# First attention stage: 16 heads in pairs on different row and column groups of TensorE

## The chip, the cores and the metric

One Trainium2 chip, one of its cores. The metric is the device time of one execution in microseconds, the median of several runs.

## What is computed

All tensors are fp32. The reference has two layers, cut here to what matters:

```python
# layer 0: x, ctx are (32, 256, 256); 16 heads of 16 features
q, k, v = x @ Wq.T, ctx @ Wk.T, ctx @ Wv.T      # split in 16 heads
att = softmax(q @ k.T * 16 ** -0.5) @ v          # per head, heads put side by side
x = x + att[0]                                   # of batch 0 alone, added to all 32
# layer 1, for each of the 32 batches
nX, nF = layernorm(ctx) * w1 + b1, layernorm(x) * w2 + b2
A = softmax(nF @ nX.T / 16) @ nX
c = gelu(A @ fc1.T + b) @ fc2.T + b
n = layernorm(c) * w3 + b3
out = nF + gamma2 * (c + gamma1 * softmax(n @ n.T / 16) @ n)
```

Of layer 0 only batch 0's attention is needed. It has 16 heads, 256 queries and 256 keys.

## The kernel before

Each engine runs a program written out by hand, and semaphores tie them together. No scheduler moves anything. There are five stages, one after the other:

- projections q, k, v of batch 0 (L700, L706);
- the first stage proper, the 16 heads of batch 0 (L719 to L755 on PE, L370 to L392 on DVE, L571 to L586 on ACT). It ends in tgt2, the attention's result;
- the second stage over 32 batches: POOL adds tgt2 to each x tile (L310) and normalizes (L317), PE transposes (L768) and multiplies (L778, L785, L794, L806);
- a short stretch on DVE (L486 to L501), then the second attention over 16 pairs of batches (L839 to L895);
- the output (L914, L554) and its stores.

In the first stage proper one head goes through five steps. **Scores**, L725: two fp32 matmuls, one for each half of the queries. The head's 16 features lie in a group of 32 partitions: heads h and h + 1 (h even) share a group, and kTm holds k twice, once with the even heads' features zeroed and once with the odd ones'. So a score matmul uses 32 rows of the array and all 128 columns. The result, 128 x 512, fills bank 3 or bank 4 of PSUM. **Maximum**, L375 on DVE, into hmax. **Exponential**, L580 on ACT, two instructions into E. **Transposes**, L735: four on PE, over the whole array, into bank 5 or 6, which then are copied to PT by ACT (L586, even heads) or DVE (L381, odd heads). **Output product**, L745: two fp32 matmuls over 128 rows and 32 columns, v1 against PT. Head h writes 32 partitions of bank 0 or 1: partition group h % 4, so the heads of a group of four lie in different column groups of the array.

PE's order sets the pace: in turn h it computes the scores of head h, the transposes of head h - 1 and the output product of head h - 2. The semaphores are s0_mm (scores ready), max0_ok, exp0_ok (two for each head), p0_mm (transposes ready), pt0_ok (two: ACT's and DVE's copy to PT done) and o0_mm (output product done). E, hmax and PT have two buffers each, one for a head.

The second attention (L881) has output products of the same form as L745: fp32, 128 rows, 32 columns, 256 columns moved. Batch 0 of a pair uses column group 0, batch 1 group 1, with a transpose (L851) between them except in the last two pairs. Its scores (L842) are bf16, and the two batches of a pair lie on rows 0 to 35 and 64 to 99 of the array.

Of the kernel before, what the change touches and what calls it, by code (L numbers as in the profile page):

```python
# [24 lines left out]
ALU = mybir.AluOpType  # L25
ACT = mybir.ActivationFunctionType
AX = mybir.AxisListType

P = 128
B = 32  # L30
N = 256
D = 256
NT = N // P
DC = D // P
TILES = B * NT
NH = 16
# [4 lines left out]
VW = 32  # L41
# [7 lines left out]
SU = 6 * U  # L49
CO = 2 * H + 2  # L50
SC = 6 * CO


COLS = {}
# [8 lines left out]
def build(nc, x, ctx, x0t, c0t, wqt, wkt, wvt, params, out):  # L63
    stack = ExitStack()

    def sb(name, shape, dt=F32):
        return stack.enter_context(nc.sbuf_tensor(name, shape, dt))
# [5 lines left out]
    bank = [stack.enter_context(nc.psum_tensor(f"bank{i}", [P, 512], F32)) for i in range(8)]  # L73

    def tiles(ap, w=256):
        return ap[:, 0:2 * w].rearrange("p (a b) -> p a b", a=2)
# [3 lines left out]
    ident = sb("ident", [P, P])  # L80
# [7 lines left out]
    qT = sb("qT", [P, 2, N])  # L88
    kTm = sb("kTm", [P, 2, 2, N])
    v1 = sb("v1", [P, NT, NH, VW])  # L90
    hmax = sb("hmax", [P, 2, NT])
    hsum = sb("hsum", [P, NT, NH])
    tgt2 = sb("tgt2", [P, NT, D])

# [11 lines left out]
    E = sb("E", [P, 2, NT * N])  # L106
    PT = sb("PT", [P, 2, NT * N])
# [37 lines left out]
    PT2 = sb("PT2", [P, 2, 2, NT * N])  # L145
# [17 lines left out]
    consts = sem("consts")  # L163
    q_mm, k_mm, v_mm = sem("q_mm"), sem("k_mm"), sem("v_mm")
    qT_ok, kT_ok, v1_ok = sem("qT_ok"), sem("kT_ok"), sem("v1_ok")
    s0_mm, max0_ok, exp0_ok = sem("s0_mm"), sem("max0_ok"), sem("exp0_ok")
    p0_mm, o0_mm = sem("p0_mm"), sem("o0_mm")
    oT_ok = [sem("oT_first"), sem("oT_second")]
    ot_mm = sem("ot_mm")
    pt0_ok = [sem("pt0_even"), sem("pt0_odd")]  # L170
# [9 lines left out]
    alg = sem("alg")  # L180
# [29 lines left out]
    def phase2(eng, step, last):  # L210
        for p in range(4):
            step(p, p % 2)
        with eng.Fori(2, PAIRS // 2 - 2) as g:
            step(g * 2, 0)
            step(g * 2 + 1, 1)
        for p in range(PAIRS - 4, last):
            step(p, p % 2)

    def paired(p, k):

# [11 lines left out]
    ALG = {}  # L232
# [90 lines left out]
    def _(dve):  # L323
# [43 lines left out]
        dve.wait_ge(qk_mm, 1)  # L367
        link(dve.tensor_copy(Q[:, :], bank[7][:, 0:(H + 1) ** 2]))
        link(dve.tensor_copy(K[:, :], bank[7][:, 64:64 + U * U]), "QK")
        for h in range(NH + 1):  # L370
            if h < NH:
                dve.wait_ge(s0_mm, h + 1)
                if h >= 2:
                    dve.wait_ge(exp0_ok, 2 * (h - 1))
                dve.tensor_reduce(hmax[:, h % 2, :], tiles(bank[3 + h % 2]), AX.X, ALU.max, negate=True)\  # L375
                    .then_inc(max0_ok, 1)
            if h >= 1 and (h - 1) % 2 == 1:
                dve.wait_ge(p0_mm, h)
                if h >= 3:
                    dve.wait_ge(o0_mm, h - 2)  # L380
                dve.tensor_copy(PT[:, (h - 1) % 2, :], bank[5 + (h - 1) % 2][:, :]).then_inc(pt0_ok[1], 1)  # L381
        dve.wait_ge(o0_mm, NH)
        dve.tensor_copy(oT[:, 1, :], bank[1][:, :]).then_inc(oT_ok[1], 1)
        dve.wait_ge(ot_mm, 1)
        for t in range(NT):
            o = bank[5 + t][:, :].rearrange("p (h k) -> p h k", h=NH)
            dve.reciprocal(hsum[:, t, :].unsqueeze(2), o[:, :, DK:DK + 1]).then_inc(hsum_ok, 1)
        for t in range(NT):
            o = bank[5 + t][:, :].rearrange("p (h k) -> p h k", h=NH)
# [172 lines left out]
    def _(act):  # L562
# [5 lines left out]
        for t in range(NT):  # L568
            act.activation(v1[:, t, :, 0:DK], bank[2][:, t * D:(t + 1) * D].rearrange("p (h k) -> p h k", h=NH),
                           ACT.Copy).then_inc(v1_ok, 1)  # L570
        for h in range(NH + 1):  # L571
            if h == 12:
                act.wait_ge(o0_mm, NH // 2)
                act.activation(oT[:, 0, :], bank[0][:, :], ACT.Copy).then_inc(oT_ok[0], 1)
            if h < NH:
                act.wait_ge(max0_ok, h + 1)
                if h >= 2:
                    act.wait_ge(p0_mm, h - 1)
                for t in range(NT):
                    act.activation(E[:, h % 2, t * N:(t + 1) * N], bank[3 + h % 2][:, t * N:(t + 1) * N], ACT.Exp,  # L580
                                   bias=hmax[:, h % 2, t:t + 1]).then_inc(exp0_ok, 1)
            if h >= 1 and (h - 1) % 2 == 0:
                act.wait_ge(p0_mm, h)
                if h >= 3:
                    act.wait_ge(o0_mm, h - 2)
                act.activation(PT[:, (h - 1) % 2, :], bank[5 + (h - 1) % 2][:, :], ACT.Copy).then_inc(pt0_ok[0], 1)  # L586

        def step(i, j, g):
            n = (j + 1) % 2
# [98 lines left out]
    def _(pe):  # L688
# [3 lines left out]
        for c in range(DC):  # L692
            last = pe.matmul(bank[6][:, 0:H + 1], meanw[:, :], a5[:, c, :], start=c == 0, stop=c == DC - 1)
        last.then_inc(mean_mm, 1)

        for arrived, n, w, src, b, done in ((q_in, 32, wqT, x0T, 0, q_mm), (k_in, 32, wkT, c0T, 1, k_mm)):
            pe.wait_ge(arrived, n)
            for o in range(2):
                for c in range(DC):
                    last = pe.matmul(bank[b][:, o * N:(o + 1) * N], w[:, c, o * P:(o + 1) * P], src[:, c, :],  # L700
                                     start=c == 0, stop=c == DC - 1)
            last.then_inc(done, 1)
        pe.wait_ge(v_in, 16)
        for t in range(NT):
            for c in range(DC):
                last = pe.matmul(bank[2][:, t * D:(t + 1) * D], c0T[:, c, t * P:(t + 1) * P], wvT[:, c, :],  # L706
                                 start=c == 0, stop=c == DC - 1)
# [3 lines left out]
        for dst, w, src, n in ((0, meanw, prodQ, (H + 1) ** 2), (64, scalew, prodK, U * U)):  # L711
            for c in range(DC):
                last = pe.matmul(bank[7][:, dst:dst + n], w[:, :], src[:, c, :], start=c == 0, stop=c == DC - 1)
# [2 lines left out]

        pe.wait_ge(qT_ok, 1)
        pe.wait_ge(kT_ok, 2)
        for h in range(NH + 2):  # L719
            if h < NH:  # L720
                o, q, e = h // 8, 32 * ((h % 8) // 2), h % 2
                if h >= 2:
                    pe.wait_ge(exp0_ok, 2 * (h - 1))
                for t in range(NT):
                    last = pe.matmul(bank[3 + h % 2][:, t * N:(t + 1) * N], qT[q:q + 32, o, t * P:(t + 1) * P],  # L725
                                     kTm[q:q + 32, e, o, :], start=True, stop=True)
                last.then_inc(s0_mm, 1)
            if 1 <= h <= NH:
                pe.wait_ge(exp0_ok, 2 * h)
                if h >= 3:  # L730
                    pe.wait_ge(pt0_ok[(h - 1) % 2], (h - 1) // 2)
                n = (h - 1) % 2
                for k in range(NT):
                    for t in range(NT):
                        last = pe.transpose(bank[5 + n][:, k * N + t * P:k * N + (t + 1) * P],  # L735
                                            E[:, n, t * N + k * P:t * N + (k + 1) * P], ident[:, :])
                last.then_inc(p0_mm, 1)
            if h >= 2:
                if h == 2:
                    pe.wait_ge(v1_ok, 2)  # L740
                    pe.wait_ge(consts, 11)
                pe.wait_ge(pt0_ok[h % 2], h // 2)
                group, row = (h - 2) // 4, VW * ((h - 2) % 4)
                for k in range(NT):
                    last = pe.matmul(bank[group // 2][row:row + VW, (group % 2) * N:(group % 2 + 1) * N],  # L745
                                     v1[:, k, h - 2, :], PT[:, h % 2, k * N:(k + 1) * N],
                                     start=k == 0, stop=k == NT - 1, skip_group_check=True)
                last.then_inc(o0_mm, 1)

        for group in range(NH // 4):  # L750
# [65 lines left out]
        for c in range(DC):  # L816
            last = pe.transpose(bank[5][:, c * P // 2:(c + 1) * P // 2].bitcast(BF16),
                                stR[:, c, :, :].rearrange("p m r -> p (m r)"), identb[:, :])
# [156 lines left out]
```

## Time and profile before

| | us |
|---|---|
| median of 3 runs | 375.85 |
| the 3 runs | 373.79, 375.85, 382.89 |
| span of the profiled execution | 371.2 |
| of it: load and projections, to 12.9 | 12.9 |
| the 16 heads, and tgt2 | 48.2 |
| second stage, to about 247 | 185.9 |
| the rest | 124.2 |

The span runs from the first instruction to the last. Of the profiled execution the profile gives the span alone, no other time, so what lies around it is the distance from the span to the three runs. A granted clock of 1.00 is 2.4 GHz on TensorE, 0.50 is 1.2 GHz.

### The profile page before, as it was taken

Reading aid. Unit: us, or ns where it says so; the run is one execution under the profiler, and the core shown is the slowest. Engines: PE = TensorE matmul, PEld = TensorE weight load, DVE = VectorE, ACT = ScalarE, POOL = GpSimd, SP = SyncE. Lnnn points to the kernel's source line nnn. Section 1 sums busy time; section 2 is a strip of 40 time slices with the busy share of each in tenths; the row PEclk is TensorE's granted clock in tenths of the full one; section 3 lists DMA queues with packets and bytes.
Section 4 is the critical chain, followed back from the end, with each engine's and each line's share of the span. In section 5 each row is a group of like instructions: output and inputs, shape, how many; then the busy total and the mean of one; then the engine's idle time right before and its main releaser. Section 6 shows DMA issues by size and latency. Waiting matters only on the chain.

```text
span 371.2 us, 6844 instructions
## 1 busy us (share of the span) xinstructions
PE 297.3 (80%) x1854; PEld 218.2 (59%) x1854; DVE 242.0 (65%) x756; ACT 166.5 (45%) x401; POOL 117.1 (32%) x183
## 2 busy tenths in 40 slices
PE   6899994277989999999999999950049999963683
PEld 5655552166879999998999899950014444421120
DVE  7534345578977778777777773239954666647685
ACT  2334430053566566666566666540054565423340
POOL 9000002664476666666667774000000000000000
PEclk9889998569699999998999899965556999995555
DMA  7300000134414445544444421100000000000798
GB/s 243 127 2 0 0 4 0 42 112 158 172 68 147 145 152 170 170 170 170 170 154 141 150 93 57 58 1 0 0 2 0 1 0 0 2 0 2 266 336 303
DMA packets 19313, 35.10 MB, mean 95 GB/s; under 512 B 2272, under 2 KB 2272, under 8 KB 19296
## 3 DMA queue, kind: packets, MB, share of 16 engines
q1 hardware_dynamic: 19296, 34.89, 26.7%
q8 instruction: 8, 0.13, 0.2%
q14 instruction: 9, 0.07, 0.1%
HBM read 18.11 MB, written 8.39 MB: 71 GB/s over the span
## 4 chain that ended last, share of the span: by engine, by line
PE 25%; issue 24%; POOL 18%; DVE 18%; DMA 10%; SPq 2%; ACT 2%; POOLq 1%; DVEq 0%; ACTq 0%
PE bank L881 7%; POOL zc L317 6%; POOL xN L310 6%; POOL zy L317 6%; DMA xN<-x 5%; DMA out<-fin 4%; PE bank L778 4%; PE bank L858 3%; PE bank L806 2%; DVE bn L427 2%; PE bank L842 2%; PE bank L768 2%; DVE fin L554 2%; PE bank L785 1%; PE bank L830 1%
## 5 line engine op out<-in xcount | busy, mean ns | idle before, releaser
L310 POOL TENSOR_TENSOR xN<-xN,tgt 128x512 f32<-128x512 f32 x32 | 40.5, 1266 | 107.8 <-DVE rstd L401 52.7
L778 PE MATMUL bank<-XT,FT 128*128 128x256 f32 x256 | 66.1, 405 | 0.0
L608 ACT ACTIVATE E<-bank,nmax 128x256 f32<-128x256 f32 x64 | 27.2, 485 | 60.9 <-DVE nmax L458 60.9
L778 PEld LDWEIGHTS bank<-XT,FT 128*128 128x128 f32 x256 | 49.9, 206 | 6.3
L596 ACT ACTIVATE FT<-bank,par 128x256 f32<-128x256 f32 x64 | 32.8, 569 | 24.6 <-PE bank L768 24.2
L427 DVE BATCH_NORM_STATS2 bn<-cN 128x6 f32<-128x256 f32 x64 | 24.1, 418 | 21.2 <-POOL xN L310 21.0
L785 PEld LDWEIGHTS bank<-fc1s,XT 128*128 128x128 f32 x256 | 34.1, 194 | 6.0 <-DVE V L463 4.2
L768 PE MATMUL bank<-ident,zc 128*128 128x128 f32 x128 | 22.2, 299 | 18.5 <-POOL zy L317 12.4
L317 POOL TENSOR_SCALAR zc<-cN,nmean,rstd 128x256 f32<-128x256 f32 x64 | 34.8, 553 | 3.6 <-DVE rstd L401 3.6
L317 POOL TENSOR_SCALAR zy<-xN,nmean,rstd 128x256 f32<-128x256 f32 x64 | 35.0, 557 | 0.0
L785 PE MATMUL bank<-fc1s,XT 128*128 128x4 f32 x256 | 31.0, 244 | 3.4 <-DVE V L463 3.4
L601 ACT ACTIVATE XT<-bank,b1s,w1s 128x256 f32<-128x256 f32 x64 | 32.9, 578 | 0.0
L806 PEld LDWEIGHTS bank<-V,PT 128*128 128x128 f32 x256 | 32.3, 198 | 0.5 <-issue 0.4
L806 PE MATMUL bank<-V,PT 128*128 128x5 f32 x256 | 31.8, 248 | 0.4 <-DVE OA L467 0.4
L881 PE MATMUL bank<-PT,uS 128*32 128x256 f32 x128 | 30.7, 401 | 0.0
L458 DVE TENSOR_REDUCE nmax<-bank 128x2 f32<-128x512 f32 x32 | 21.9, 684 | 10.9 <-PE bank L778 9.3
L375 DVE TENSOR_REDUCE hmax<-bank 128x2 f32<-128x512 f32 x16 | 11.1, 691 | 26.2 <-PE bank L725 26.1
L515 DVE TENSOR_REDUCE nm<-bank 128x2 bf16<-128x512 f32 x32 | 20.6, 685 | 11.2 <-PE bank L842 11.2
L768 PEld LDWEIGHTS bank<-ident,zc 128*128 128x128 f32 x128 | 16.0, 161 | 20.0 <-POOL zy L317 16.0
L830 PE MATMUL bank<-identb,sU 128*128 128x128 bf16 x64 | 7.2, 243 | 24.8 <-ACT sU L630 24.8
L554 DVE TENSOR_TENSOR fin<-bank,Fall 128x512 f32<-128x512 f32 x32 | 21.4, 690 | 7.6 <-DMA out<-fin 4.6
L580 ACT ACTIVATE E<-bank,hmax 128x256 f32<-128x256 f32 x32 | 13.4, 470 | 25.7 <-DVE hmax L375 25.7
(150 smaller groups left out, 494.2 us busy)
## 6 DMA issues: line engine op xcount, KB each, us to landing
cN<-ctx SPq DMA_DIRECT2D x32, 256.0 KB, 2.6
xN<-x SPq DMA_DIRECT2D x32, 256.0 KB, 2.9
Fall<-FT SPq DMA_DIRECT2D x32, 256.0 KB, 3.0
out<-fin SPq DMA_DIRECT2D x32, 256.0 KB, 2.1
x0T<-x0t SPq DMA_DIRECT2D x1, 256.0 KB, 2.7
wqT<-wqt SPq DMA_DIRECT2D x1, 256.0 KB, 2.9
c0T<-c0t SPq DMA_DIRECT2D x1, 256.0 KB, 3.5
wkT<-wkt SPq DMA_DIRECT2D x1, 256.0 KB, 4.8
```

Of the source, the lines that this page charges most:

```text
L310: pool.tensor_tensor(xN[:, slot, :], xN[:, slot, :], tgt2[:, :, :].rearrange("p t d -> p (t d)"), ALU.add).then_inc(y_ok, 1)
L317: pool.tensor_scalar(dst[:, zslot, cols], src[:, zslot, cols], nmean[:, pair, k:k + 1], rstd[:, pair, k:k + 1], ALU.add, ALU.mult).then_in ...
L427: dve.bn_stats(bn[:, pr, m, t, :], src[:, slot, (t % NT) * D:(t % NT + 1) * D]).then_inc(bn_ok, 1)
L554: dve.tensor_tensor(fin[:, j, :], bank[j][:, :], Fall[:, bass.ds(g * (4 * DC * N) + j * DC * N, DC * N)], ALU.add).then_inc(fin_ok, 1)
L596: act.activation(FT[:, n, c, :], bank[1][:, c * N:(c + 1) * N], ACT.Identity, bias=c_("b2", c), scale=c_("w2", c)).then_inc(FT_ok, 1)
L601: act.activation(XT[:, n, c, :], bank[0][:, c * N:(c + 1) * N], ACT.Identity, bias=b1s[:, c:c + 1], scale=w1s[:, c:c + 1]).then_inc(XT_ok, 1)
L608: act.activation(E[:, j % 2, t * N:(t + 1) * N], bank[2 + j % 2][:, t * N:(t + 1) * N], ACT.Exp, bias=nmax[:, j % 2, t:t + 1]).then_inc(ex ...
L768: last = pe.transpose(bank[b][:, c * N + t * P:c * N + (t + 1) * P], z[:, (j + 1) % 4, t * D + c * P:t * D + (c + 1) * P], ident[:, :])
L778: last = pe.matmul(bank[2 + j % 2][:, t * N:(t + 1) * N], FT[:, j % 2, c, t * P:(t + 1) * P], XT[:, j % 2, c, :], start=c == 0, stop=c == ...
L785: last = pe.matmul(bank[6][:, t * H:(t + 1) * H], XT[:, j % 2, c, t * P:(t + 1) * P], fc1[:, c, :], start=c == 0, stop=c == DC - 1)
L806: last = pe.matmul(bank[7][:, t * (H + 1):(t + 1) * (H + 1)], PT[:, j % 2, k * N + t * P:k * N + (t + 1) * P], V1[:, (j + 2) % 4, k, :], s ...
L881: last = pe.matmul(bank[6][VW * m:VW * (m + 1), 0:N], uS[:, 1 - r, m, k, :], PT2[:, 1 - r, m, k * N:(k + 1) * N], start=k == 0, stop=k == ...
```

## The change

The 16 heads are taken as eight pairs, HP: (0,2), (4,6), (1,3), (5,7), and the same plus 8. The heads of a pair lie in different groups of 32 partitions (0 and 32, or 64 and 96), so their score matmuls use different rows of the array, and their output products different columns (partition groups 0 and 2, or 1 and 3, of the same bank). PE's turn p is now: scores of pair p, transposes of pair p - 1, output product of pair p - 2. Within scores and output product the matmuls alternate between the two heads.

Scores have four banks, two for each pair: 3 and 4, 2 and 7. Bank 2 held the v projection and bank 7 the products for Q and K, so waits for v1_ok and for Q and K come ahead of the first scores. The exponentials have four buffers: the two of E, and two of PT2, which lies idle until the second attention. The transposes' banks 5 and 6 and PT have one buffer for each head of a pair: ACT copies the first head's, DVE the second's. o0_mm and s0_mm count pairs.

```diff
+HP = [(8 * o + 2 * i + e, 8 * o + 2 * i + e + 2) for o in range(2) for e in range(2) for i in (0, 2)]
+NHP = len(HP)
...
+    def EH(n):
+        return E[:, n, :] if n < 2 else PT2[:, 0, n - 2, :]
+
+    SBANK = ((bank[3], bank[4]), (bank[2], bank[7]))
...
+        for p in range(NHP + 1):
+            if p < NHP:
+                dve.wait_ge(s0_mm, p + 1)
+                if p >= 2:
+                    dve.wait_ge(exp0_ok, 4 * (p - 1))
+                for m in range(2):
+                    dve.tensor_reduce(hmax[:, 2 * (p % 2) + m, :], tiles(SBANK[p % 2][m]), AX.X, ALU.max, negate=True)\
+                        .then_inc(max0_ok, 1)
+            if p >= 1:
+                dve.wait_ge(p0_mm, 2 * p)
+                if p >= 2:
+                    dve.wait_ge(o0_mm, p - 1)
+                dve.tensor_copy(PT[:, 1, :], bank[6][:, :]).then_inc(pt0_ok[1], 1)
...
+        for p in range(NHP + 1):
+            if p == 6:
+                act.wait_ge(o0_mm, NHP // 2)
                 act.activation(oT[:, 0, :], bank[0][:, :], ACT.Copy).then_inc(oT_ok[0], 1)
...
+            if p < NHP:
+                for m in range(2):
+                    act.wait_ge(max0_ok, 2 * p + m + 1)
+                    if p >= 2:
+                        act.wait_ge(p0_mm, 2 * (p - 1))
+                    n = 2 * (p % 2) + m
+                    for t in range(NT):
+                        act.activation(EH(n)[:, t * N:(t + 1) * N], SBANK[p % 2][m][:, t * N:(t + 1) * N], ACT.Exp,
+                                       bias=hmax[:, n, t:t + 1]).then_inc(exp0_ok, 1)
+            if p >= 1:
+                act.wait_ge(p0_mm, 2 * p - 1)
+                if p >= 2:
+                    act.wait_ge(o0_mm, p - 1)
+                act.activation(PT[:, 0, :], bank[5][:, :], ACT.Copy).then_inc(pt0_ok[0], 1)
...
+        pe.wait_ge(v1_ok, 2)
+        pe.wait_ge(alg, ALG["QK"])
+        for p in range(NHP + 2):
+            if p < NHP:
+                if p >= 2:
+                    pe.wait_ge(exp0_ok, 4 * (p - 1))
                 for t in range(NT):
...
+                    for m, h in enumerate(HP[p]):
+                        o, q, e = h // 8, 32 * ((h % 8) // 2), h % 2
+                        last = pe.matmul(SBANK[p % 2][m][:, t * N:(t + 1) * N], qT[q:q + 32, o, t * P:(t + 1) * P],
+                                         kTm[q:q + 32, e, o, :], start=True, stop=True)
                 last.then_inc(s0_mm, 1)
...
+            if 1 <= p <= NHP:
+                if p >= 2:
+                    pe.wait_ge(pt0_ok[0], p - 1)
+                    pe.wait_ge(pt0_ok[1], p - 1)
+                for m in range(2):
+                    pe.wait_ge(exp0_ok, 4 * (p - 1) + 2 * (m + 1))
+                    n = 2 * ((p - 1) % 2) + m
+                    for k in range(NT):
+                        for t in range(NT):
+                            last = pe.transpose(bank[5 + m][:, k * N + t * P:k * N + (t + 1) * P],
+                                                EH(n)[:, t * N + k * P:t * N + (k + 1) * P], ident[:, :])
+                    last.then_inc(p0_mm, 1)
+            if p >= 2:
+                if p == 2:
+                    pe.wait_ge(consts, 11)
+                for m in range(2):
+                    pe.wait_ge(pt0_ok[m], p - 1)
                 for k in range(NT):
...
+                    for m, h in enumerate(HP[p - 2]):
+                        group, row = h // 4, VW * (h % 4)
+                        last = pe.matmul(bank[group // 2][row:row + VW, (group % 2) * N:(group % 2 + 1) * N],
+                                         v1[:, k, h, :], PT[:, m, k * N:(k + 1) * N],
+                                         start=k == 0, stop=k == NT - 1, skip_group_check=True)
                 last.then_inc(o0_mm, 1)
```

On PE, in the middle of the stage, two turns before (L725 scores, L735 transposes, L745 output product):

```order
L725 MATMUL bank4<-kTm,qT 128x256 [waits exp0_ok]
L725 MATMUL bank4<-kTm,qT 128x256
L735 MATMUL bank5<-ident,E 128x128 [waits pt0_even,exp0_ok]
L735 MATMUL bank5<-ident,E 128x128 x3
L745 MATMUL bank0<-PT,v1 32x256 [waits pt0_odd]
L745 MATMUL bank0<-PT,v1 32x256
L725 MATMUL bank3<-kTm,qT 128x256 [waits exp0_ok]
L725 MATMUL bank3<-kTm,qT 128x256
L735 MATMUL bank6<-ident,E 128x128 [waits pt0_odd,exp0_ok]
L735 MATMUL bank6<-ident,E 128x128 x3
L745 MATMUL bank1<-PT,v1 32x256 [waits pt0_even]
```

And one turn of the change on PE (L738, L750 and L761 are the same three steps):

```order
L738 MATMUL bank3<-kTm,qT 128x256 [waits exp0_ok]
L738 MATMUL bank4<-kTm,qT 128x256
L738 MATMUL bank3<-kTm,qT 128x256
L738 MATMUL bank4<-kTm,qT 128x256
L750 MATMUL bank5<-ident,PT2 128x128 [waits exp0_ok,pt0_odd,pt0_even]
L750 MATMUL bank5<-ident,PT2 128x128 x3
L750 MATMUL bank6<-ident,PT2 128x128 [waits exp0_ok]
L750 MATMUL bank6<-ident,PT2 128x128 x3
L761 MATMUL bank0<-PT,v1 32x256 [waits pt0_odd,pt0_even]
L761 MATMUL bank0<-PT,v1 32x256 x3
```

Two heads' scores stand together and alternate between banks, eight transposes follow, and both of them and the output product wait for both copies, ACT's and DVE's, where before each waited for one.

On ACT, two heads of the stage before (L580 exponential, L586 copy to PT):

```order
L580 ACTIVATE E<-bank3,hmax 128x256 [waits p0_mm,max0_ok]
L580 ACTIVATE E<-bank3,hmax 128x256
L580 ACTIVATE E<-bank4,hmax 128x256 [waits p0_mm,max0_ok]
L580 ACTIVATE E<-bank4,hmax 128x256
L586 ACTIVATE PT<-bank5 128x512 [waits o0_mm,p0_mm]
```

And one pair of the change on ACT (L590, L596):

```order
L590 ACTIVATE PT2<-bank2,hmax 128x256 [waits p0_mm,max0_ok]
L590 ACTIVATE PT2<-bank2,hmax 128x256
L590 ACTIVATE PT2<-bank7,hmax 128x256 [waits p0_mm,max0_ok]
L590 ACTIVATE PT2<-bank7,hmax 128x256
L596 ACTIVATE PT<-bank5 128x512 [waits o0_mm,p0_mm]
```

The order on ACT reads alike; but the four exponentials now belong to one pair and depend on scores that come together, and the copy behind them is of the pair before.

## Rows read from the trace of the kernel before

**Rows 1.** Window of the stage: busy us of PE, PEld, DVE, ACT, POOL, granted clock, DMA.

```profile
12.90:61.10 48.20, 45.81 (x200) 25.21 (x200) 17.99 (x31) 17.85 (x41) 0.00 (x0) 0.93 0.00 1
```

**Rows 2.** Timeline, one head of the steady part: start us, us, engine, line, what.

```profile
42.75 1.13 PE L725 MATMUL bank<-kTm,qT 32*128 32x256 f32 x4
43.81 0.66 PE L735 MATMUL bank<-ident,E 128*128 128x128 f32 x4
43.91 0.69 DVE L375 TENSOR_REDUCE hmax<-bank 128x2 f32<-128x512 f32 x1 [1.34 <-PE bank L725]
44.39 1.05 PE L745 MATMUL bank<-PT,v 128*32 128x256 f32 x4
44.64 0.84 ACT L580 ACTIVATE E<-bank,hmax 128x256 f32<-128x256 f32 x2 [1.79 <-DVE hmax L375]
45.37 0.60 ACT L586 ACTIVATE PT<-bank 128x512 f32<-128x512 f32 x1
45.37 1.13 PE L725 MATMUL bank<-kTm,qT 32*128 32x256 f32 x4
```

**Rows 3.** Who waited for whom, from 13 to 61 us: us in total, times, longest.

```profile
ACT E L580 <- DVE hmax L375: 25.7, 15, 3.1
```

**Rows 4.** Timeline, the end of the stage and the seam to the next.

```profile
56.61 1.90 PE L745 MATMUL bank<-PT,v 128*32 128x256 f32 x8
61.12 2.49 POOL L310 TENSOR_TENSOR xN<-xN,tgt 128x512 f32<-128x512 f32 x2 [51.96 <-DVE tgt L391]
```

**Rows 5.** The chain that ended last, its first long piece: start us, us, what.

```profile
4.04 5.35 DMA xN<-x
```

**Rows 6.** Timeline, the start of the stage.

```profile
12.97 0.20 DVE L369 COPY K<-bank 128x36 f32<-128x36 f32 x1
12.99 1.96 PE L725 MATMUL bank<-kTm,qT 32*128 32x256 f32 x8 [0.37 <-DVE kTm L366]
14.93 1.63 ACT L580 ACTIVATE E<-bank,hmax 128x256 f32<-128x256 f32 x4 [2.42 <-DVE hmax L375]
15.82 1.12 PE L735 MATMUL bank<-ident,E 128*128 128x128 f32 x4 [0.86 <-ACT E L580]
16.86 2.07 PE L725 MATMUL bank<-kTm,qT 32*128 32x256 f32 x4
18.86 1.12 PE L735 MATMUL bank<-ident,E 128*128 128x128 f32 x4
19.91 1.92 PE L745 MATMUL bank<-PT,v 128*32 128x256 f32 x4
21.76 1.13 PE L725 MATMUL bank<-kTm,qT 32*128 32x256 f32 x4
```

**Rows 7.** Timeline of PE, second attention: matmuls in shared and in different groups.

```profile
324.06 0.61 PE L858 MATMUL bank<-nm2T,sel 4*128 4x256 bf16 x4
324.60 0.40 PE L842 MATMUL bank<-sT 36*128 36x256 bf16 x4
...
325.29 1.05 PE L881 MATMUL bank<-PT,uS 128*32 128x256 f32 x4
...
328.37 1.06 PE L881 MATMUL bank<-PT,uS 128*32 128x256 f32 x8
```

**Rows 8.** Timeline of PE, eight transposes in a row in the second stage.

```profile
81.84 0.66 PE L768 MATMUL bank<-ident,zc 128*128 128x128 f32 x4 [0.38 <-POOL zy L317]
...
82.34 0.60 PE L768 MATMUL bank<-ident,zy 128*128 128x128 f32 x4
```

**Rows 9.** Windows around the granted clock's changes (columns as in rows 1).

```profile
15.00:21.00 6.00, 5.18 (x15) 3.13 (x16) 2.06 (x3) 2.99 (x7) 0.00 (x0) 0.50 0.00 0
22.00:60.00 38.00, 37.67 (x176) 20.43 (x175) 13.96 (x22) 14.79 (x34) 0.00 (x0) 1.00 0.01 1
72.00:79.00 7.00, 4.93 (x19) 4.33 (x20) 4.52 (x22) 2.92 (x7) 3.93 (x6) 0.50 0.57 187
80.00:88.00 8.00, 7.62 (x55) 7.10 (x54) 7.58 (x23) 2.77 (x6) 5.17 (x9) 1.00 0.48 165
```

More of the change, by code:

```diff
@@ L90, in build @@
     v1 = sb("v1", [P, NT, NH, VW])
-    hmax = sb("hmax", [P, 2, NT])
+    hmax = sb("hmax", [P, 4, NT])
     hsum = sb("hsum", [P, NT, NH])
@@ L369, in _ @@
         link(dve.tensor_copy(K[:, :], bank[7][:, 64:64 + U * U]), "QK")
[L370 to L382, printed above, removed]
+        for p in range(NHP + 1):
[11 more added lines that the diff above has]
+                dve.tensor_copy(PT[:, 1, :], bank[6][:, :]).then_inc(pt0_ok[1], 1)
+        dve.wait_ge(o0_mm, NHP)
         dve.tensor_copy(oT[:, 1, :], bank[1][:, :]).then_inc(oT_ok[1], 1)
@@ L570, in _ @@
                            ACT.Copy).then_inc(v1_ok, 1)
-        for h in range(NH + 1):
-            if h == 12:
-                act.wait_ge(o0_mm, NH // 2)
+        for p in range(NHP + 1):
+            if p == 6:
+                act.wait_ge(o0_mm, NHP // 2)
                 act.activation(oT[:, 0, :], bank[0][:, :], ACT.Copy).then_inc(oT_ok[0], 1)
[L575 to L586, printed above, removed]
+            if p < NHP:
[12 more added lines that the diff above has]
+                act.activation(PT[:, 0, :], bank[5][:, :], ACT.Copy).then_inc(pt0_ok[0], 1)
         def step(i, j, g):
@@ L718, in _ @@
         pe.wait_ge(kT_ok, 2)
[L719 to L723, printed above, removed]
+        pe.wait_ge(v1_ok, 2)
[4 more added lines that the diff above has]
+                    pe.wait_ge(exp0_ok, 4 * (p - 1))
                 for t in range(NT):
-                    last = pe.matmul(bank[3 + h % 2][:, t * N:(t + 1) * N], qT[q:q + 32, o, t * P:(t + 1) * P],
-                                     kTm[q:q + 32, e, o, :], start=True, stop=True)
+                    for m, h in enumerate(HP[p]):
+                        o, q, e = h // 8, 32 * ((h % 8) // 2), h % 2
+                        last = pe.matmul(SBANK[p % 2][m][:, t * N:(t + 1) * N], qT[q:q + 32, o, t * P:(t + 1) * P],
+                                         kTm[q:q + 32, e, o, :], start=True, stop=True)
@@ L727, in _ @@
                 last.then_inc(s0_mm, 1)
[L728 to L732, printed above, removed]
-                for k in range(NT):
[L734 to L747, printed above, removed]
+            if 1 <= p <= NHP:
[10 more added lines that the diff above has]
+                    last.then_inc(p0_mm, 1)
```

## Prediction

> **What bounds the kernel now.** I read the windows by stage first. The first stage, from 12.9 to 61.1 us, keeps PE busy for 45.81 of 48.20 us at a granted clock of 0.93, while DVE and ACT are busy for 18 us each and no data moves [rows 1]. Then the timeline of one head in the steady part: its scores start at 42.75, its transposes (of the head before) at 43.81, the output product (of the head before that) at 44.39, and the next head's scores at 45.37 [rows 2]. So a head costs 1.06 + 0.58 + 0.98 = 2.62 us of PE without a gap. The list of waits says the same from the other side: ACT waits 25.7 us for the maxima, and these hang on L725, the scores [rows 3]. PE's own order of work is the bound. Last, the seam to the second stage: the last output product ends at 56.61 + 1.90 = 58.51, and POOL, which had sat idle for 51.96 us, starts its first addition at 61.12, released by tgt2 [rows 4]. Its tiles had landed long before: in the chain that ended last, the x transfer lands at 4.04 + 5.35 = 9.39 [rows 5]. So each us that the first stage gives back moves all that follows forward by one.
>
> **Can matmuls of two heads overlap? The rows that price it.** An fp32 matmul leaves two records. On the same rows and columns of the array each record costs a slot: eight score records took 1.96 us [rows 6] where four took 1.13 [rows 2], 0.21 a slot. The second attention (L881) already has what the change brings for the output product: fp32, 128 rows by 32 columns, two batches in different column groups. With a transpose between the batches four records take 1.05 us; at the stage's end, where nothing stands between, eight take 1.06 [rows 7]. The second batch is free, and this although its records stand behind all four of the first in the program. For row groups the nearest rows are bf16: four matmuls of 256 columns on the same rows (L858) take 0.61 us, four of the same size on two halves of the rows (L842) 0.40 [rows 7]. A third of the time fell away, which fits two pairs side by side. I take the same for fp32 scores in row groups of 32; the bounds are free (1.07 us for a pair) and fully serial (1.06 + 4 x 0.21 = 1.92).
>
> **The pair's cost on PE.** Scores 1.06 + 0.01. Transposes use the whole array and gain only that their fixed part comes once for two heads: the two groups zc and zy, eight transposes, run from 81.84 to 82.94, 1.10 us against 0.66 for four, so four more cost 0.44, and the pair's transposes 0.58 + 0.44 = 1.02 [rows 8]. Output product 0.98 + 0.01. Sum 3.08 us a pair against 5.24 for two heads: 2.16 less.
>
> **Does PE stay the bound?** ACT now does four exponentials before it copies a half of the pair before, and the transposes of the pair wait for that copy (pt0_ok), since bank 5 and bank 6 are single. Behind that wait on PE stand the transposes and the output product, and next the scores that DVE waits for. From the end of the scores: DVE starts 0.03 later (43.88 to 43.91), the first exponential 0.73 after that (43.91 to 44.64) [rows 2], four exponentials take 1.63 [rows 6], the copy starts 0.11 before the last one's recorded end and takes 0.60, hand-over 0.04: 2.92 us. DVE's second maximum is ready after 2 x 0.69, before ACT wants it, and its own copy waits for the output product, which ends about 2.0 after the scores, so it is done at 2.7. On PE the same stretch is -0.07 + 1.02 + 0.99 + 1.07 = 3.01. The chain fits with 0.09 to spare, and what it might lack is paid half (a wait before the transposes moves the next scores, too). This is the wait that is late next. The Trainium skill ("TensorEngine Tiling (Array Packing)", section PSUM Bottleneck) warns that tiling speeds up TensorE but not the evacuation of PSUM. For load the rows give room, ACT 1.63 + 0.60 and DVE 3 x 0.69 in 3.08 us; on latency they bear the warning out, though by it alone the sum stays as it is.
>
> **The start.** The waits for v1 and for Q and K now stand ahead of the first scores. K's copy ends at 12.97 + 0.20 = 13.17, so the scores start at 13.2 instead of 12.99: 0.2 lost [rows 6]. The granted clock was 0.50 (1.2 GHz) from 15 to at least 21 and 1.00 (2.4 GHz) from 22 on [rows 9], and I keep these times. Pair 0's scores 13.2 to 14.35, pair 1's to 15.2; exponentials from 15.1, the last of pair 0 done at 16.75; second half of the transposes at 16.8, and 1.04 after it (as 15.82 to 16.86) pair 2's scores at 17.85. At half clock scores take 2.00 (16.86 to 18.86) and transposes 1.05 + 0.86 (18.86 to 19.91, and double the 0.44 as an estimate), so transposes 19.85, output product 21.75 [rows 6]. Clock back: scores of pair 3 at 22.75.
>
> **Steady part and tail.** Four periods of 3.08 bring pair 7's scores to 35.05, ending at 36.2. Now the chain shows, as no scores fill in: transposes of pair 7 at 36.2 + 2.92 = 39.1, output product of pair 6 at 40.1 to 41.2, DVE's copy (taken at its maximum's 0.69, the same 512 columns) and 0.04 twice, output product of pair 7 at 41.95 to 43.0. ACT's copy of oT (0.6) falls in ACT's gap of 3.08 - 2.1 and costs nothing; without that cover it would cost about 0.3. The end was 58.51: **15.5 us gained**. Everything after the seam is taken as it was (312.7 us). DMA issues and POOL's and SP's programs are untouched.
>
> The profiled execution has a span of 371.2; the three times are 373.79, 375.85 and 382.89, so the median lies 4.65 above it. Span after: 355.7. Median after: 375.85 - 15.5 = 360.3.
>
> **Rivals.**
> 1. *Starts in program order.* If a record can't start before its predecessors in the program, the two records of one matmul hold up the other head's: A1; A2 with B1; B2 with A1'; A2' with B1'; B2' are five slots for eight records, not four. That is 0.21 for scores and 0.21 for the output product, 0.43 a pair, 3.4 in all: 363.7. Against it speaks L881, where a whole batch of records was overtaken [rows 7]. The Trainium skill ("TensorE: Matmul & The Clock Gate", Part 3) has this rule: matmuls keep program order in start and end, and by it the time would be this one. The L881 row doesn't agree with it for column groups; for fp32 row groups no row speaks. 12%.
> 2. *fp32 scores of different row groups run one after the other.* Four more slots a pair, 0.86 x 8 = 6.9: 367.2. For: only bf16 rows show this overlap, and one score matmul loads 128 fp32 columns of weights for each record. Against: L842. 8%.
> 3. *The change doesn't do what it says:* alternating brings no overlap at all, and only three of six changes of step a pair (scores to transposes to output product) are saved. Scores and output product serial, 2 x 0.86 x 8 = 13.8 back: 374. Against: [rows 7]. 3%.
> 4. *The clock stays at half, and the kernel gets slower.* The first stage's PE packs the same work into fewer busy slots; should the granted clock not return at 22 but stay at 0.5 through the stage, a pair costs 2.00 + 1.91 + 1.85 (19.91 to 21.76) = 5.76 [rows 6], worse than 5.24. Over 7 pairs 7 x (5.76 - 3.08) = 18.8 is lost against 15.5: 379. It decides from about six pairs at half clock on. Against: with pairs and overlap, PE still has next to no gap in the steady part, and the stage's only cold stretch begins where PE waited, from 12.99 + 1.96 = 14.95 to 15.82 [rows 6]. 2%.
> 5. *Part of the gain comes back later.* The second stage starts 15.5 us earlier; there PE started at half clock and got the full one at about 80 [rows 9]. If that cold stretch lasts 8 us longer, 8 us at half clock do 4 us of work, and at most 4 come back: 364.3. Cut shorter, it gives up to 4: 356.3. The seam's other work hangs on POOL and DVE, whose clocks don't change. 8%.
>
> **How the numbers follow.** The forecast has 67%: 360.3, with 357 to 363 for the cold start, the chain and the spread of the three times. The range takes in the program-order rival, the serial scores and the later loss, 356.5 to 367.5, and leaves out rivals 3 and 4 and the ends of that spread. About 2% is what a measurement of this kernel can tell from no change, here 368.3 and 383.4. Below 368.3 lie the forecast, rivals 1, 2 and 5: 95%, of which I give one up to what no case here names; within 2% rival 3 and most of rival 4: 5%; slower 1%.
>
> **What would show it.** Scores of a pair: eight records in about 1.15 us, start to the transposes 1.07 (rival 1: 1.28; rival 2: 1.9). Output product: eight in 1.07. Period of a pair 3.08 to 3.2, from the starts of the scores. PE's wait for ACT's copy before the transposes: under 0.1 in the steady part, about 1 us once at the end. The first POOL addition on xN at 45.6 instead of 61.12. Wrong would be: a pair's period near 3.9, a clock under 1.00 after 22 us, or a second stage that doesn't keep its 312.7 us.

## The result, and the profile after

| | before | after |
|---|---|---|
| median of 4 runs, us | 374.82 (373.05 to 382.89) | 358.69 (357.86 to 359.12) |
| ratio, 95% interval | | 0.9582 (0.9543 to 0.9622) |
| span of the profiled execution | 371.2 | 356.0 |

The kernel is 4.2% faster. Ratios and intervals leave out runs with a lower granted clock and a time over 1.5% above the fastest (here 382.89 us, before), medians don't; without it the median before is 373.79. The windows of the stage, to the first POOL addition, and of its parts at either clock (us of PE, PEld, DVE, ACT, POOL, then granted clock and DMA), answer to [rows 1, 9]:

```profile
12.90:47.10 34.20, 28.68 (x206) 18.23 (x205) 17.86 (x31) 17.54 (x43) 0.00 (x0) 0.90 0.01 2
17.00:23.00 6.00, 6.00 (x26) 4.49 (x28) 2.84 (x5) 3.87 (x11) 0.00 (x0) 0.50 0.00 0
24.00:45.00 21.00, 19.14 (x150) 11.70 (x148) 11.75 (x18) 11.95 (x28) 0.00 (x0) 1.00 0.01 2
```

In these windows the stage is 14 us shorter. The same instructions ran on DVE and ACT for the same 18 us; PE's busy time fell from 45.8 to 28.7 us although it executes as many matmuls. The granted clock was 0.50 for 6.8 us in both profiles, from 15.0 to 21.8 before and from 16.6 to 23.4 after. The timeline of one pair in the steady part answers to [rows 2]:

```profile
30.23 1.13 PE L738 MATMUL bank<-kTm,qT 32*128 32x256 f32 x8
30.51 0.61 ACT L596 ACTIVATE PT<-bank 128x512 f32<-128x512 f32 x1
31.30 1.09 PE L750 MATMUL bank<-ident,E 128*128 128x128 f32 x8
31.41 1.29 DVE L383 TENSOR_REDUCE hmax<-bank 128x2 f32<-128x512 f32 x2 [0.30 <-PE bank L738]
32.14 1.57 ACT L590 ACTIVATE PT<-bank,hmax 128x256 f32<-128x256 f32 x4 [1.02 <-DVE hmax L383]
32.32 1.06 PE L761 MATMUL bank<-PT,v 128*32 128x256 f32 x8
33.31 1.13 PE L738 MATMUL bank<-kTm,qT 32*128 32x256 f32 x8
```

Eight score records take 1.13 us, as long as four did, and eight output records 1.06, against 1.05 for four. Steps start 1.07, 1.02 and 0.99 apart: a pair costs 3.08 us, and two heads cost 5.24 before. Reductions in a row are 0.60 apart here, not 0.69. ACT's copy ends at 30.51 + 0.61 = 31.12 and the transposes start at 31.30, just when PE is free for them. The start answers to [rows 6]:

```profile
14.14 1.16 PE L738 MATMUL bank<-kTm,qT 32*128 32x256 f32 x16 [0.60 <-DVE K L376]
16.99 1.97 PE L750 MATMUL bank<-ident,E 128*128 128x128 f32 x8 [1.69 <-ACT E L590]
18.89 2.08 PE L738 MATMUL bank<-kTm,qT 32*128 32x256 f32 x8
20.90 1.97 PE L750 MATMUL bank<-ident,PT 128*128 128x128 f32 x8
22.80 1.35 PE L761 MATMUL bank<-PT,v 128*32 128x256 f32 x8
24.09 1.13 PE L738 MATMUL bank<-kTm,qT 32*128 32x256 f32 x8
```

Pairs 0 and 1 lie in four different row groups, and all their sixteen records, issued one behind the other, are through in 1.16 us. It gains nothing here, since the transposes wait for the exponentials until 16.99. And the tail, with the seam [rows 4]:

```profile
38.47 1.06 PE L761 MATMUL bank<-PT,v 128*32 128x256 f32 x8
40.43 1.07 PE L750 MATMUL bank<-ident,PT 128*128 128x128 f32 x8 [0.91 <-ACT PT L596]
42.60 0.69 DVE L389 COPY PT<-bank 128x512 f32<-128x512 f32 x1 [2.27 <-PE bank L761]
43.44 1.06 PE L761 MATMUL bank<-PT,v 128*32 128x256 f32 x8 [0.95 <-DVE PT L389]
47.11 2.48 POOL L317 TENSOR_TENSOR xN<-xN,tgt 128x512 f32<-128x512 f32 x2 [37.96 <-DVE tgt L399]
```

Where the 15.2 us of the span came from: first scores to last output product took 58.51 - 12.99 = 45.52 us and take 44.50 - 14.14 = 30.36, 15.2 less. The stage starts 1.15 later: PE's products for K end at 12.92 + 0.61 = 13.53 instead of 12.62, in a part that the change doesn't touch, and PE then stands for 0.60 us, now for K's copy, where it stood for 0.37. What follows the last output product takes 311.5 us against 312.7, which makes up for it. That difference need not be the change's: in the profiles of all the kernels below it lies between 310.5 and 312.9 us.

The second stage meets half clock again [rows 9]. Its stretch at 0.50 is as long as before, 17 us, first before, then after:

```profile
62.80:79.80 17.00, 5.74 (x21) 5.01 (x22) 11.09 (x53) 3.73 (x8) 9.00 (x13) 0.50 0.23 77
```

```profile
50.80:67.80 17.00, 7.76 (x28) 6.67 (x29) 10.87 (x51) 3.86 (x8) 10.21 (x16) 0.50 0.22 77
```

### The profile page after: what moved, and what is told of

Read it like the earlier page. It is cut to its first block, busy times and chain, and to the rows that moved or that the text cites. A ratio compares the mean times of both kernels' runs of the same rounds, so it can differ in the third digit from the quotient of the medians.

```text
span 356.0 us, 6835 instructions
## 1 busy us (share of the span) xinstructions
PE 280.2 (79%) x1854; PEld 210.8 (59%) x1854; DVE 241.7 (68%) x756; ACT 165.6 (47%) x401; POOL 117.1 (33%) x183
## 4 chain that ended last, share of the span: by engine, by line
PE 23%; issue 22%; POOL 20%; DVE 18%; DMA 11%; SPq 2%; ACT 2%; POOLq 1%; DVEq 0%; ACTq 0%
PE bank L897 8%; POOL zc L324 7%; POOL zy L324 7%; DMA xN<-x 7%; POOL xN L317 7%; DMA out<-fin 4%; PE bank L874 3%; PE bank L794 2%; DVE bn L435 2%; PE bank L858 2%; PE bank L822 2%; DVE fin L562 2%; PE bank L846 1%; DVE big L486 1%; PE bank L888 1%
## 5 line engine op out<-in xcount | busy, mean ns | idle before, releaser
L794 PE MATMUL bank<-XT,FT 128*128 128x256 f32 x256 | 64.9, 400 | 0.0
L606 ACT ACTIVATE FT<-bank,par 128x256 f32<-128x256 f32 x64 | 32.8, 569 | 22.2 <-PE bank L784 21.8
L784 PE MATMUL bank<-ident,zc 128*128 128x128 f32 x128 | 21.9, 297 | 18.1 <-POOL zy L324 12.3
L435 DVE BATCH_NORM_STATS2 bn<-xN 128x6 f32<-128x256 f32 x64 | 23.5, 409 | 0.0
L654 ACT ACTIVATE PT<-bank 128x512 f32<-128x512 f32 x32 | 17.4, 595 | 12.6 <-PE bank L874 12.6
```

Source lines behind the costliest of these rows:

```text
L435: dve.bn_stats(bn[:, pr, m, t, :], src[:, slot, (t % NT) * D:(t % NT + 1) * D]).then_inc(bn_ok, 1)
L606: act.activation(FT[:, n, c, :], bank[1][:, c * N:(c + 1) * N], ACT.Identity, bias=c_("b2", c), scale=c_("w2", c)).then_inc(FT_ok, 1)
L784: last = pe.transpose(bank[b][:, c * N + t * P:c * N + (t + 1) * P], z[:, (j + 1) % 4, t * D + c * P:t * D + (c + 1) * P], ident[:, :])
L794: last = pe.matmul(bank[2 + j % 2][:, t * N:(t + 1) * N], FT[:, j % 2, c, t * P:(t + 1) * P], XT[:, j % 2, c, :], start=c == 0, stop=c == ...
```

## The experiments

All start from the changed kernel unless said otherwise. In tables, period is from one pair's scores to the next pair's at full clock, and stage from the first scores to the end of the last output product in the profiled execution.

### Which overlap gives how much: the pairs chosen otherwise

Heads h and h + 1 share rows; heads h, h + 4, h + 8 share columns. Three choices of pairs take away one overlap, the other, and both, and leave the order of steps as it is, the half as many changes of step among it. With the same columns, alone or with the rows, bank 0 is complete only at the end, so there ACT's copy of oT moves behind the last pair. From the end of the last output product to POOL's first addition it is then 2.95 us instead of 2.61.

```diff
-HP = [(8 * o + 2 * i + e, 8 * o + 2 * i + e + 2) for o in range(2) for e in range(2) for i in (0, 2)]
+HP = [(2 * i, 2 * i + 1) for i in range(8)]                                   # same rows
+HP = [(h, (h + 12) % 16 if h < 4 else h + 4) for h in range(8)]               # same columns
+HP = [(h, h + 8) for h in range(8)]                                           # same both
...
# same columns and same both
-            if p == 6:
-                act.wait_ge(o0_mm, NHP // 2)
-                act.activation(oT[:, 0, :], bank[0][:, :], ACT.Copy).then_inc(oT_ok[0], 1)
...
+        act.wait_ge(o0_mm, NHP)
+        act.activation(oT[:, 0, :], bank[0][:, :], ACT.Copy).then_inc(oT_ok[0], 1)
```

> Pairs (0,1), (2,3), ...: the two heads of a pair use the same 32 rows for the scores and different columns for the output product. My theory, that the gain comes from matmuls that run side by side in both steps: eight score records take 1.9 us instead of 1.13 and the period of a pair goes from 3.07 to 3.93. With one score step at half clock (1.7 more) and five at full clock (0.86 each), and 0.8 at the start, 6.8 us come back: about 365.5 us. Rival, that the gain comes from changing step half as often: the period stays at 3.07, about 359.

> Pairs (0,12), (1,13), (2,14), (3,15), (4,8), ...: different rows for the scores, the same column group (in banks 0 and 1) for the output product. ACT's copy of oT moves to the end of the stage, since bank 0 is complete only then. My theory: eight output records take 1.9 us instead of 1.06, the period of a pair is 3.93, 7.5 pairs of 0.86 and some at half clock and 0.45 for the late copy: about 7.8 us come back, 366.5 us. Rival, fewer changes of step: the period stays at 3.07, 359.2.

> Pairs (0,8), (1,9), ...: the same rows and the same column group in both steps, so pairing is left and nothing can run side by side; oT's late copy as in the run with the same columns. My theory: both losses add, period 4.79, about 14.2 us come back, 373 us, 2 us less than the kernel before for half as many changes of step (0.45 us for a pair of 5.24). Rival, fewer changes of step: 359.2.

| pairs share | period | us, median | ratio to the kernel before |
|---|---|---|---|
| nothing (the change) | 3.08 | 358.69 | 0.9582 (0.9543 to 0.9622) |
| rows | 3.93 | 367.11 | 0.9805 (0.9702 to 0.9907) |
| columns | 3.93 | 366.3 | 0.979 (0.9744 to 0.9836) |
| both | 4.79 | 373.48 | 0.9982 (0.9949 to 1.0015) |

PE's timeline of a pair, with the same rows:

```profile
35.59 1.99 PE L738 MATMUL bank<-kTm,qT 32*128 32x256 f32 x8
37.51 1.09 PE L750 MATMUL bank<-ident,E 128*128 128x128 f32 x8
38.53 1.06 PE L761 MATMUL bank<-PT,v 128*32 128x256 f32 x8
```

With the same columns:

```profile
33.26 1.13 PE L737 MATMUL bank<-kTm,qT 32*128 32x256 f32 x8
34.33 1.09 PE L749 MATMUL bank<-ident,E 128*128 128x128 f32 x8
35.35 1.91 PE L760 MATMUL bank<-PT,v 128*32 128x256 f32 x8
37.19 1.13 PE L737 MATMUL bank<-kTm,qT 32*128 32x256 f32 x8
```

And with both:

```profile
38.85 1.99 PE L737 MATMUL bank<-kTm,qT 32*128 32x256 f32 x8
40.77 1.09 PE L749 MATMUL bank<-ident,E 128*128 128x128 f32 x8
41.79 1.91 PE L760 MATMUL bank<-PT,v 128*32 128x256 f32 x8
```

Each step is slow exactly where its groups are shared, by 0.85 us, and the losses add. The last two forecasts were met within 0.5 us. With the same rows the four times were 364.77, 364.78, 369.45 and 376.62; their median lies 1.6 us over the 365.5 expected, the middle one of the three that enter the ratio (the first three) 0.7 under it. With nothing side by side, pairing alone can't be told from the kernel before (0.9982, and 1.0 is in the interval), so the rival "fewer changes of step" falls as the main cause. It is 0.45 us a pair in the periods (4.79 to 5.24); that profile had the half clock for 13.7 us of the stage, though, against 6.8 before, and oT's copy comes later, so how much of the 0.45 reaches the end isn't shown. The profiles with the same rows and with the same columns had it for 10.2 us, which is in their times too; the periods, all read at full clock, are free of it. Practically the whole gain is overlap, about half in the scores and half in the output products.

### Does the alternating order matter?

```diff
-                for t in range(NT):
-                    for m, h in enumerate(HP[p]):
+                for m, h in enumerate(HP[p]):
+                    for t in range(NT):
```

and the same for the output product's loops over k and m.

> The changed kernel, with the matmuls of a pair in the order head by head and not alternating: both score matmuls of the first head, then both of the second, and the same for the output product. My theory, that an array group takes its next matmul whatever the order between groups: eight records still take 1.06 to 1.13 us, the period stays at 3.07, 358.7 us within 0.5. Rival, that starts keep program order: the second head's first record starts with the first head's fourth, seven slots for eight records, 0.65 us more in each of the two steps of eight pairs, 10 us: 369.

It takes 358.33 us, ratio 0.9561 (0.9497 to 0.9625). PE's timeline of a pair:

```profile
30.29 1.14 PE L738 MATMUL bank<-kTm,qT 32*128 32x256 f32 x8
31.36 1.09 PE L750 MATMUL bank<-ident,E 128*128 128x128 f32 x8
32.38 1.06 PE L761 MATMUL bank<-PT,v 128*32 128x256 f32 x8
```

Head by head is as fast. The first 0.2 us of the scores, asked for alone, already hold two records:

```profile
30.29 0.49 PE L738 MATMUL bank<-kTm,qT 32*128 32x256 f32 x2
```

A record doesn't name its head. But in one group records start 0.21 us or more apart, so the second of the two must be the second head's first, fifth in the program. With starts in program order seven slots were expected, 0.65 us more a step. That order is refuted for row and for column groups in fp32; that the matmuls "alternate" is no part of the gain, that they lie in different groups is all of it.

### How near is the chain on ACT and DVE?

```diff
                     for t in range(NT):
+                        if m == 1 and t == 1:
+                            act.activation(big[:, p * N:(p + 1) * N], SBANK[p % 2][m][:, t * N:(t + 1) * N], ACT.Exp,
+                                           bias=hmax[:, n, t:t + 1])
                         act.activation(EH(n)[:, t * N:(t + 1) * N], SBANK[p % 2][m][:, t * N:(t + 1) * N], ACT.Exp,
```

> A fifth exponential for each pair on ACT, ahead of the fourth and into an idle tile, lengthens the chain scores, maximum, exponentials, copy to PT, transposes by 0.36 us. In the changed kernel ACT's copy ends 0.18 us before the transposes start, 0.14 without the hand-over. My theory: the chain then lacks 0.22 us, PE waits half of it each turn, the period of a pair goes from 3.07 to 3.18, and with the tail the kernel takes 1.2 us more, about 359.9. Rival one, that PE has more room: period 3.07, only the tail's 0.4 us more. Rival two, that the lack is paid in full: period 3.29, 2.0 us more.

It takes 359.32 us, ratio 0.9597 (0.9551 to 0.9643): by the time alone not to be told from the change. The trace tells it. PE's scores and transposes, with ACT's copy, in two turns:

```profile
33.06 1.13 PE L741 MATMUL bank<-kTm,qT 32*128 32x256 f32 x8
33.68 0.62 ACT L599 ACTIVATE PT<-bank 128x512 f32<-128x512 f32 x1
34.36 1.09 PE L753 MATMUL bank<-ident,E 128*128 128x128 f32 x8 [0.17 <-ACT PT L599]
36.37 1.13 PE L741 MATMUL bank<-kTm,qT 32*128 32x256 f32 x8
36.76 0.62 ACT L599 ACTIVATE PT<-bank 128x512 f32<-128x512 f32 x1
37.44 1.09 PE L753 MATMUL bank<-ident,PT 128*128 128x128 f32 x8
39.45 0.92 PE L741 MATMUL bank<-kTm,qT 32*128 32x256 f32 x6
```

The copy now ends at 34.30 and 37.38, and the transposes start 0.06 behind it. In the first turn they start 1.30 after the scores, in the second 1.07: the periods alternate between 3.31 (33.06 to 36.37) and 3.08 (36.37 to 39.45), 3.19 on average, where 3.18 was expected. One turn's wait gives the next turn its slack; that is the half that is paid. The fifth exponential lengthens the chain by 0.36 us, and PE waits 1.30 - 1.07 = 0.23 of it. So the chain had 0.13 us of room in the changed kernel, and this chain from the scores to ACT's copy is the next bound. Half clock lasted 13.7 us in this profile, which moves the time by more than the wait does.

### Can more be merged?

Sixteen score records in 1.16 us suggest steps of four heads. First the scores of two pairs in one step every other turn:

```diff
-            if p < NHP:
-                if p >= 2:
-                    pe.wait_ge(exp0_ok, 4 * (p - 1))
+            if p < NHP and p % 2 == 0:
+                if p >= 2:
+                    pe.wait_ge(exp0_ok, 4 * p)
                 for t in range(NT):
+                    for r in (p, p + 1):
...
```

> The scores of two pairs, four row groups of 32, in one step every other turn. Sixteen records took 1.16 us at the start of the changed kernel, so PE saves 1.07 us for two pairs. My theory: the chain is then the bound. From the end of the scores to ACT's copy of the pair before 2.82, hand-over 0.04, transposes 1.02 and output product 0.99 of the second turn and scores 1.17: about 6.0 us for two pairs against 6.14, 0.3 us in all, 358.4. Rival, that PE alone is the bound: 5.07 for two pairs, 355.5.

It takes 356.63 us, ratio 0.9534 (0.95 to 0.9568); the stage in its profile is 44.25 - 13.82 = 30.43 us, no shorter than the change's 30.36. Two pairs take 6.21 us. The timeline:

```profile
26.95 1.15 PE L739 MATMUL bank<-kTm,qT 32*128 32x256 f32 x16
29.05 1.06 PE L763 MATMUL bank<-PT,v 128*32 128x256 f32 x8
30.22 0.69 DVE L389 COPY PT<-bank 128x512 f32<-128x512 f32 x1 [0.81 <-PE bank L763]
30.83 1.28 DVE L383 TENSOR_REDUCE hmax<-bank 128x2 f32<-128x512 f32 x2
31.01 1.07 PE L752 MATMUL bank<-ident,E 128*128 128x128 f32 x8 [0.91 <-DVE PT L389]
31.54 1.56 ACT L590 ACTIVATE PT<-bank,hmax 128x256 f32<-128x256 f32 x4 [0.64 <-DVE hmax L383]
33.16 1.15 PE L739 MATMUL bank<-kTm,qT 32*128 32x256 f32 x16
```

The sixteen records are as cheap as hoped, and all of it goes to the chain, as the theory had it. It takes 0.17 more than expected. By the timeline that is DVE's order: it copies first, at 30.22, and the second pair's maxima stand behind that copy although their scores have been ready since 28.1. No run has them the other way round. The median is 2 us under the change's of another set of runs; the stage's profile gives no reason for it, and it wasn't repeated.

Then two buffers of PT, with ACT's copy between the exponentials of the two heads (run twice), and on top of it the output products of two pairs in one step (run twice), and that merging only for the last four pairs:

```diff
+    def PTH(m, p):
+        return PT[:, m, :] if p % 2 == 0 else PT2[:, 1, m, :]
...
-                if p >= 2:
-                    dve.wait_ge(o0_mm, p - 1)
-                dve.tensor_copy(PT[:, 1, :], bank[6][:, :]).then_inc(pt0_ok[1], 1)
+                if p >= 3:
+                    dve.wait_ge(o0_mm, p - 2)
+                dve.tensor_copy(PTH(1, p - 1), bank[6][:, :]).then_inc(pt0_ok[1], 1)
...
+# output products of four heads, and for the last four pairs only
+HP = [(8 * o + a, 8 * o + a + 2) for o in range(2) for a in (0, 5, 4, 1)]
...
# output products of four heads
-            if p >= 2:
+            if p >= 3 and p % 2 == 1:
...
+                    for r in (p - 3, p - 2):
+# only for the last four pairs
+            for rs in (((p - 2,),) if 2 <= p < 6 else ((p - 3, p - 2),) if p >= 6 and p % 2 == 1 else ()):
```

> PT gets two buffers for each head of a pair (the second in the idle half of PT2), so that copies no longer wait for the output product of the pair before, and ACT copies between the exponentials of the first and the second head. PE's order is that of the change. My theory: PE is the bound, the period stays at 3.07, and only the tail gets shorter, by 0.5 before the last transposes and up to 0.75 before the last output product: 357.5. Rival, that the copies' waits cost something each turn: period under 3.05, 356.5 or less.

> As the run with two buffers of PT, and the output products of two pairs, four column groups of 32, in one step every other turn, with pairs (0,2), (5,7), (4,6), (1,3). PE saves 0.99 us for two pairs. My theory: in the turn without an output product the transposes wait about 0.3 us for the chain, so two pairs take 5.5 us against 6.14, 2 us less than with two buffers alone: 355.5. Rival one, the chain takes all of it back: 6.1 for two pairs, 357.5. Rival two, four column groups don't run side by side in fp32: two pairs take 6.1 as well, with sixteen output records in 1.9 us instead of 1.1.

> The changed kernel once more, beside the next one on the same chip. 358.7 us, and a half-clock stretch of some 6 to 7 us in the stage.

> Two buffers of PT once more. The first run's profile had the stage 2.6 us shorter than the changed kernel's, 1.5 of it in the tail and 1.1 in a shorter half-clock stretch. My theory: the tail's 1.5 us are there every time and the rest is chance, so 1.5 us less than the changed kernel beside it. Rival: it isn't faster by more than 0.5 us.

> Output products of four heads once more. The first run's profile had the granted clock at 0.50 from 17 to 36 us with PE busy for 18.96 of 19 us. Theory: with the steps of two pairs merged the clock stays low, and the stretch is again longer than 12 us. Rival: that was chance; the stretch is 6 to 8 us as in the changed kernel and the span about 353.

> Two buffers of PT, the pairs (0,2), (5,7), (4,6), (1,3), and the output products of pairs 4 and 5 and of 6 and 7 alone in one step; the first four pairs as in the change. If the merged steps keep the clock from coming back, they are absent here while it is low, so the half-clock stretch is 6 to 7 us and the merged steps run at 1.00 behind it: 0.9 us less than with two buffers alone at most, 357. Rival, that merged steps pull the clock down whenever they come: 0.50 again from pair 4 on, 360 or more.

| kernel | us, median | ratio to before | stage | of it at half clock |
|---|---|---|---|---|
| the change | 358.69 | 0.9582 | 30.4 | 6.8 |
| the change again | 358.13 | 0.9522 (0.9485 to 0.9558) | 33.3 | 13.7 |
| two buffers of PT | 357.89 | 0.9572 (0.9541 to 0.9603) | 27.7 | 3.4 |
| two buffers again | 359.47 | 0.9559 (0.9519 to 0.9598) | 28.8 | 6.8 |
| outputs of four | 359.79 | 0.96 (0.9567 to 0.9634) | 33.4 | 20.5 |
| outputs of four again | 360.91, one run | | 33.4 | 20.5 |
| outputs of four, last pairs only | 357.64 | 0.9536 (0.9481 to 0.959) | 29.1 | 6.8 |

In the profile the two buffers do what the theory said: the period stays at 3.08, and between profiles with the same 6.8 us at half clock the stage is 30.4 - 28.8 = 1.6 us shorter, 1.5 of it in the tail. From pair 7's scores to the end it takes 6.61 us (36.63 to 43.24) instead of 8.12, as the last eight transposes and both last output products now follow closely:

```profile
39.92 1.39 PE L753 MATMUL bank<-ident,PT 128*128 128x128 f32 x8
41.24 2.00 PE L764 MATMUL bank<-PT,v 128*32 128x256 f32 x16
```

But beside the change on the same chip the median isn't lower (359.47 to 358.13; the intervals of the ratios overlap), so the 1.5 us expected there didn't show. The time at half clock, 3.4 to 13.7 us from one profile of these two kernels to the next, moves the stage by up to 3 us and can hide it. Of the change, run again, 6 to 7 us of it had been expected. So no version is shown to be better than the change.

With the merged output products 355.5 us was expected, and 359.79 came. They did save PE time: at half clock two pairs took 9.68 us (scores at 18.93 and 28.61), against 2 x 5.76 = 11.52 in the second profile of the change (18.29 to 24.05). That nothing of it is left in the time has another cause than the chain. Windows of the stretch at half clock, in the first and in the second run:

```profile
17.00:36.00 19.00, 18.96 (x87) 13.06 (x88) 8.82 (x14) 9.57 (x24) 0.00 (x0) 0.50 0.00 1
```

```profile
17.10:37.30 20.20, 20.15 (x96) 13.55 (x100) 8.84 (x14) 9.78 (x24) 0.00 (x0) 0.50 0.00 1
```

PE was busy without a gap and kept 1.2 GHz for 20 us, both times. With the merging left to the last pairs the stretch has its 6.8 us, and the merged steps behind it run at full clock:

```profile
35.55 1.13 PE L741 MATMUL bank<-kTm,qT 32*128 32x256 f32 x8
36.75 1.39 PE L753 MATMUL bank<-ident,E 128*128 128x128 f32 x8
38.06 1.07 PE L765 MATMUL bank<-PT,v 128*32 128x256 f32 x16
```

```profile
24.00:45.00 21.00, 18.54 (x156) 11.39 (x152) 11.17 (x19) 11.48 (x27) 0.00 (x0) 1.00 0.01 2
```

Sixteen output records in 1.07 us: four column groups run side by side in fp32. Merged steps didn't pull the clock down once it was up; where they stood in a stretch at half clock, it lasted three times as long as in the change's first profile, and half as long again as in its second. What makes the difference is open: two profiles of the one and one of the other, and nothing here shows what the throttle weighs. The mean granted clock of each whole run is on record too: 0.823 in both profiled runs with 20 us, and 0.802, 0.826, 0.835, 0.835 and 0.841 in the other five of the same kernel. So the long stretch is perhaps not there every time.

## Why the prediction was right

The forecast was 360.3 us, and 358.69 was measured; the span 355.7, and 356.0 was measured. The mechanism was right. That the span came within 0.3 us is partly luck: the last output product was to end at 43.0 and ended at 44.50, and 1.2 of these 1.5 us came back in what follows it, where nothing was forecast. By its steps:

- **PE's order is the bound, and the seam passes the gain on.** Right. POOL's first addition waits for tgt2 as before, and what follows took 311.5 us, taken as 312.7.
- **fp32 output products overlap** (from L881) and **fp32 scores do too** (from the bf16 rows of L842). Both right, 1.06 and 1.13 us for eight records, and the pairs with shared groups show them as the cause.
- **A pair's cost of 3.08.** Met to the hundredth, and so the four periods: 12.29 us from 24.09 to 36.38, forecast 12.3.
- **The chain fits with 0.09 to spare, a lack is paid half.** The fifth exponential measured 0.13 of room, and that half is paid. DVE's reductions in a row are quicker than I took them (0.60 for 0.69), and ACT's four exponentials too (1.57 for 1.63).
- **The start.** From the first scores to pair 3's 9.95 us, forecast 9.55: I had kept the clock's times, but the stretch at half clock, as long as before, began at 16.6 instead of 15.0 and ended at about 23.4, not 21.75. K's copy ended at 14.00 instead of 13.17, which no step had, and the first scores came at 14.14 instead of 13.2. I took the scores of pairs 0 and 1 one after the other, and they overlapped; it was covered by the wait for the exponentials.
- **The tail.** 8.1 us from pair 7's scores, forecast 7.95.
- **Rivals.** Program order (12%) fell in the profile after and again head by head. So did serial fp32 scores (8%), whose price of 0.86 a pair the pairs with the same rows confirm (3.93 - 3.08 = 0.85). "Brings no overlap" was priced 374, and the kernel that really has none took 373.5. The clock rival didn't decide, but what I held against it was no reason: I argued that a PE without gaps gets its clock back, and in the merged output products a PE without gaps stayed at half clock for 20 us. The change itself had 6.8 us of it in one profile and 13.7 in another; the runs' medians were about the same. Of the later loss in the second stage nothing is seen: its half-clock stretch was 17 us long, as before, and the time from POOL's first addition to the end 308.9 us against 310.1.

- **From span to median.** Sized wrong. I took 4.65 us, the distance from the span to a median of three, one of them the 382.89. In the runs on record a span lies 1.7 to 1.9 us under its own time, so the profiled execution, with 371.2, was most likely the 373.05, the quickest of the four; the rest of the 4.65 was spread. After the change the distance is 2.69, which is 1.96 less, and with the 0.3 that the span is over, that is the 1.6 us by which the forecast was too high. The medians lie 16.1 us apart only with the 382.89; without it they lie 15.1 apart, as the spans do with 15.2.

## What to carry to other kernels

Small fp32 matmuls that use 32 rows or 32 columns of the array were as good as free in pairs here, and up to four at once, when they lay in different row or column groups: 1.06 to 1.16 us for eight or sixteen records, against 1.05 to 1.13 for four. The row groups wrote to different banks and the column groups to different partitions; nothing else was run. Lay the data out so that neighbours in the program differ in this way; their order within the step made no difference. Look for rows in the trace where it already happens by chance, as in the last turns of a later stage here, and price the change by them. Then work out the chain on the engines that empty PSUM, since a further merge of PE's steps can end there, as that of the scores did (6.21 us for two pairs against 6.15).

## What was not expected of the hardware

- Sixteen fp32 score records in four row groups took 1.16 us, sixteen output records in four column groups 1.07, four of either in one group 1.13 and 1.05.
- Between groups a matmul starts ahead of those that stand before it in the program: the same 1.14 and 1.06 us when all of one head's records stand ahead of the other's.
- The granted clock stayed at 0.50 for 20 us with PE busy 18.96 of 19 us. The stretch after the stage's first scores lasted 3.4 to 20 us in different profiles, 6.8 and 13.7 with the same kernel, and this is the largest part of what differs between two profiles of the same stage (30.4 and 33.3 us).
